# Attention scores of a whole tile as 16 products in four 32-row strips, in a cross-attention and quantized-FFN kernel

## What is computed

```python
x = x + xattn(layernorm(x), ctx, ctx, mask, wq, bq, wk, bk, wv, bv, wo, bo)
#   Q, K, V: 16 heads of 32; scores = Q K^T / sqrt(32)
#   scores = where(mask == 0, 1e-9, scores); softmax over the 120 keys
#   (softmax @ V) @ wo + bo
x = x + ffn(layernorm(x), w1, b1, w2, b2)
#   bitlinear(x, w, b) = act_quant(rmsnorm(x)) @ weight_quant(w).T + b
#   ffn: bitlinear -> gelu (exact) -> bitlinear
```

## Time and profile before

| | us |
|---|---|
| median of 3 runs (lowest, highest) | 778.81 (778.54, 779.88) |
| the profiled execution | 776.87 |
| its span from first to last instruction | 774.9 |
| PE, DVE, ACT, POOL busy in it | 709.6, 607.8, 527.4, 542.0 |

### The profile page before, as it was taken

The page is one execution under the profiler, slowest core; times in us unless marked ns, Lnnn a source line. Parts: engine busy times, 40 slices in busy tenths (PEclk is TensorE's granted clock), DMA queues, the critical chain, the costliest instruction groups (busy, mean ns, idle before and its releaser), DMA issues.

```text
span 774.9 us, 12445 instructions
## 1 busy us (share of the span) xinstructions
PE 709.6 (92%) x4027; PEld 441.5 (57%) x4088; DVE 607.8 (78%) x1061; ACT 527.4 (68%) x1455; POOL 542.0 (70%) x677
## 2 busy tenths in 40 slices
PE   7867889899999999999999999999999999888885
PEld 6535666546665566556655566556655566444532
DVE  4595996887868897797868897797878877888784
ACT  2445456876787777777787777767687777877550
POOL 3274568756885679766886679766886668777765
PEclk9978999999999999999999999999999999999999
DMA  9941210224123422325113522324113322222234
GB/s 308 366 177 69 68 47 22 61 35 127 29 63 74 129 62 63 61 49 129 37 53 74 129 63 62 72 42 125 48 51 65 63 62 62 62 61 63 56 74 108
DMA packets 109199, 65.28 MB, mean 84 GB/s; under 512 B 90776, under 2 KB 90776, under 8 KB 108496
## 3 DMA queue, kind: packets, MB, share of 16 engines
q1 hardware_dynamic: 108079, 64.49, 31.8%
q10 hardware_dynamic: 1056, 0.00, 0.1%
HBM read 35.12 MB, written 8.39 MB: 56 GB/s over the span
## 4 chain that ended last, share of the span: by engine, by line
PE 61%; DVE 18%; POOL 7%; DMA 5%; issue 5%; ACT 3%; SPq 0%; DVEq 0%; POOLq 0%; ACTq 0%
PE ps_a L385 20%; PE ps_y L494 9%; PE ps_s L433 8%; PE ps_z L481 8%; PE ps_a L415 6%; PE ps_t L440 4%; DVE xnT_l L776 2%; PE ps_a L452 2%; DVE hid L852 2%; DMA q_hT<-q_h 2%; DMA x<-in_L_xattn_wo_dram 2%; DVE yw L836 2%; POOL prob L1101 2%; POOL hid L1108 1%; DVE ps_s L813 1%
## 5 line engine op out<-in xcount | busy, mean ns | idle before, releaser
L1101 POOL TENSOR_TENSOR prob<-prob,pinv 128x480 f32<-128x480 f32 x128 | 126.4, 987 | 169.6 <-DVE pinv L821 169.6
L670 ACT ACTIVATE prob<-ps_s,nmax 128x120 f32<-128x120 f32 x512 | 178.5, 369 | 14.9 <-DVE nmax L816 14.5
L494 PE MATMUL ps_y<-w2T,q_hT 128*128 128x512 bf16 x452 | 115.9, 379 | 12.6 <-DVE x L871 4.5
L433 PE MATMUL ps_s<-kblk,qT 128*128 128x480 f32 x256 | 125.0, 570 | 0.0
L481 PE MATMUL ps_z<-w1T,q_xT 128*128 128x512 bf16 x449 | 117.0, 379 | 4.3 <-DVE hid L852 1.3
L813 DVE COPY_PREDICATED_SCALAR ps_s<-hidden_key,masked_c 128x480 f32 x128 | 90.5, 707 | 30.1 <-PE ps_s L433 28.9
L670 ACT ACTIVATION_READ_ACCUMULATOR prob<-ps_s,nmax 128x1 f32 x512 | 109.4, 214 | 0.0
L440 PEld LDWEIGHTS ps_t<-ident,prob 128*120 128x120 f32 x512 | 62.2, 138 | 75.0 <-issue 55.2
L852 DVE SCALAR_TENSOR_TENSOR hid<-ps_z,y_deq,b_row 128x512 f32<-128x512 f32 x120 | 89.4, 745 | 7.1 <-PE ps_z L481 3.9
L641 ACT COPY probT<-ps_t 120x512 f32<-120x512 f32 x128 | 76.8, 600 | 19.0 <-PE ps_t L440 19.0
L816 DVE TENSOR_REDUCE nmax<-ps_s 128x4 f32<-128x480 f32 x128 | 84.1, 657 | 4.4
(11 more groups left out here) (150 smaller groups left out, 1488.3 us busy)
## 6 DMA issues: line engine op xcount, KB each, us to landing
xn<-in_x_dram SPq DMA_DIRECT2D x8, 1024.0 KB, 7.4
x<-in_x_dram SPq DMA_DIRECT2D x32, 256.0 KB, 2.7
out_dram<-x SPq DMA_DIRECT2D x32, 256.0 KB, 2.3
hid<-in_L_ffn_w_dram SPq DMA_DIRECT2D x4, 1024.0 KB, 9.5
w2T<-in_L_ffn_w_dram SPq DMA_DIRECT2D x2, 1024.0 KB, 14.4
ctx_k<-in_ctx_dram SPq DMA_DIRECT2D x8, 240.0 KB, 6.4
ctx_k<-in_mask_Bx1xSxS_ik_dram SPq DMA_DIRECT2D x7, 240.0 KB, 3.0
wk_s<-in_L_xattn_wk_dram SPq DMA_DIRECT2D x1, 1024.0 KB, 8.9
```

What stands on the lines that cost most here:

```text
L433: nc.tensor.matmul(ps_s[n % 3][:, 0:GK], qT[:, k % QR, g], kblk[:, g], start=True, stop=True).then_inc(s["sc_full"], 1)
L494: last = nc.tensor.matmul(y_bank(k)[:], q_hT[:, k % 2, f], w2T[:, f], start=(f == 0), stop=(f == KF - 1))
L670: last = nc.scalar.activation(prob[:, n % 3, i * S2:(i + 1) * S2], ps_s[n % 3][:, i * S2:(i + 1) * S2], ACT.Exp, bias=nmax[:, n % 4, i:i + ...
L1101: gp.tensor_tensor(pr, pr, pinv[:, n % 4].unsqueeze(2).to_broadcast([P, HG, S2]), ALU.mult).then_inc(s["prob_ready"], 1)
```

## The change

The scores of all four units of a tile are made at once, by 16 products: product (g, i) has the 32 rows of head 4g + i of the queries as its stationary operand and the same 32 rows of `keyT` as the moving one (120 columns), and writes into bank `ps_s[i]`. So a unit is now one head out of each of the four groups, there are four score banks, and `kblk`, `own_head` and `spread_keys` are gone; `keyT` has two buffers. To free a bank, the probabilities have one transpose bank `ps_t`, and x, c and k are turned in `ps_y`, between the down products of two tiles. `scores(k)` waits for the exponentials of the tile before.

```diff
-            def scores(n):
-                k, g = divmod(n, G)
-                wait(pe, "k_ready", G * (n // U) + g + 1)
+            def scores(k):
+                a = k // T
+                wait(pe, "keyT_ready", a + 1)
                 if k % T == 0:
-                    wait(pe, "a_evac", AJ_ACT[("q", k // T, g)] + 1)
-                wait(pe, "exp_done", n - 2)
-                nc.tensor.matmul(ps_s[n % 3][:, 0:GK], qT[:, k % QR, g], kblk[:, g], start=True, stop=True
-                                 ).then_inc(s["sc_full"], 1)
+                    wait(pe, "a_evac", AJ_ACT[("q", a, G - 1)] + 1)
+                wait(pe, "exp_done", G * k)
+                for g in range(G):
+                    for i in range(HG):
+                        rows = slice(i * HD, (i + 1) * HD)
+                        last = nc.tensor.matmul(ps_s[i][:, g * S2:(g + 1) * S2], qT[rows, k % QR, g],
+                                                keyT[rows, a % 2, g], start=True, stop=True)
+                last.then_inc(s["sc_full"], 1)
...
-    LOAD0, BO0, ATT0, WO0, RES0, LN20, RX0 = 2, 5, 7, 8, 9, 10, 11
-    UP0, B20, GELU0, SQ0, ABS0, QH0, DOWN0, HF0, YOUT0 = 13, 12, 16, 17, 17, 18, 20, 20, 24
+    LOAD0, BO0, ATT0, LOW0, WO0, RES0, LN20, RX0, B20 = 2, 6, 7, 8, 9, 10, 11, 12, 13
+    UP0, GELU0, SQ0, ABS0, QH0, HF0, DOWN0, YOUT0 = 14, 17, 18, 18, 19, 21, 22, 24
...
+            turns = {-3: ("c", 0), 0: ("x", 0), 1: ("x", 1), 4: ("x", 2), 5: ("x", 3), 8: ("k", 0)}
+            proj = {2: ("k", 0), 6: ("v", 0), 8: ("q", 0), 10: ("q", 1), 12: ("q", 2), 14: ("q", 3)}
+            stats, norm = ((-4, -3), (-2, -1)) if b == 2 else ((-8, -7), (-6, -4))
...
-        ps_s = [psum(f"ps_s{i}", [P, CH]) for i in range(3)]
-        ps_t = [psum(f"ps_t{i}", [P, CH]) for i in range(2)]
+        ps_s = [psum(f"ps_s{i}", [P, CH]) for i in range(HG)]
+        ps_t = psum("ps_t", [P, CH])
...
             def slot(n):
+                k = tile_at(n, ATT0)
+                if k is not None:
+                    attend(k)
+                if n >= LAG:
                     turn_probs(n - LAG)
...
+                if n >= UP0:
                     ffn_up((n - UP0) // FC, (n - UP0) % FC)
+                if n in PROJ:
...
                 k = tile_at(n, WO0)
                 if k is not None:
                     project_out(k)
+                if n % G == 0:
+                    scores(n // G)
...
+                if n in TURNS:
...
+                for half in range(2):
+                    k = tile_at(n, DOWN0 + half)
+                    if k is not None:
+                        ffn_down(k, half)
```

453 lines of the change are left out of this document (209 added, 244 removed).

## The result

| | before | after |
|---|---|---|
| median (lowest, highest), 4 runs each | 778.67 (776.66, 779.88) us | 830.88 (828.81, 832.88) us |
| span of the profiled execution | 774.9 us | 827.0 us |
| mean granted clock in it | 0.982 | 0.959 |

The ratio is 1.067, with a 95% interval of 1.064 to 1.070: the changed kernel is slower by 52 us. The forecast was 802, so 23 slower: right in sign, inside its range by 1 us, and less than half of the size.

The account below looks back on a forecast made before the run. PE was taken to bound the kernel before, a loop of ACT, PE and DVE the changed one: 774.9 us span, +19 for six sequences, +4 at the start, 798; +4 for the median's scale gives 802, range 752 to 832.

Parts of the forecast that it names:

- that ring: Loop through ACT's, PE's and DVE's queues from one tile's scores to the next's: 90.0 us a sequence against 86.8.

Follow-up runs that it names:

- e9: The changed kernel with ACT's read-out of the projection of a tile's third slot moved ahead of the square; 836.4 us.

## What to carry to other kernels

When a change makes several engines hand over at one point (four banks filled at once, where three in turn seem to let the queues drift), write down for every engine, the one with slack too, what stands in its queue between what it waits for and what it is waited for; work saved on the busiest engine is worth little as long as that ring is longer. Then move the work nobody waits for (here a layernorm and a square) behind or ahead of the link, one queue at a time, and look after each move which two instructions now meet. Here an instruction of 2 us on POOL held a subtraction on DVE for up to 2 us; cut it where DVE is the one that is late, and leave it whole where POOL is. And when two versions differ, compare their time at half clock before putting the difference down to the move.

## What was not expected of the hardware

- DVE's subtraction from SBUF to SBUF ended 0.28 us after the end of POOL's rounding instruction each time, whatever was left of that; 0.49 us alone, up to 2.10 beside it in e9. DVE's reduction right behind it kept its 0.69 us. POOL's instructions kept their 1.97 and 1.90 us.
- POOL's rounding instruction in four quarters takes 2.8 us in place of 1.97.
- The granted clock fell to half about once in a sequence, where PE's waits were no longer than 2.7 us each, and filling one or two of these waits with idle work moved the stretch by 17 us and more without taking it away.
